# Packed expert and batch numbers, read once and taken apart in registers, in a top-2 MoE kernel

## The reference

```python
out = einsum('btc,oc->bto', x, W_base) + b_base
h = einsum('btc,erc->bter', x, As)
x = x + out + 2.0 * einsum('bter,eor,be->bto', h, Bs, cond_8)

rw = softmax(cond_8); w, sel = top_k(rw, 2); w = w / w.sum(-1)
dense_w = zeros((B, E)).at[arange(B)[:, None], sel].add(w)
mlp = lambda x, g, u, d: (gelu(x @ g) * (x @ u)) @ d      # 128 -> 512 -> 128
x = x + sum_e dense_w[:, e] * mlp(x, gate[e], up[e], down[e]) + mlp(x, shared_gate, shared_up, shared_down)
```

## Time and profile before

| | us |
|---|---|
| median of three runs | 134.96 |
| the profiled execution, its own time | 135.5 |
| its span in the trace | 133.8 |
| TensorE busy in the span | 127.2 (95%) |
| VectorE busy | 88.7 (66%) |
| ScalarE busy | 70.9 (53%) |
| GpSimd busy | 60.2 (45%) |

### The profile page before, as it was taken

How to read it: one execution, slowest core, us unless ns; L and a number is a source line. 1 busy time by engine, 2 the same in 40 slices (tenths; PEclk the granted TensorE clock), 3 DMA queues, 4 the chain that set the end, 5 groups by cost and what they waited for, 6 DMA issues and landing times.

```text
span 133.8 us, 3280 instructions
## 1 busy us (share of the span) xinstructions
PE 127.2 (95%) x869; PEld 114.2 (85%) x869; DVE 88.7 (66%) x172; ACT 70.9 (53%) x134; POOL 60.2 (45%) x110
## 2 busy tenths in 40 slices
PE   6899999999999989996999999999999999999991
PEld 6658787878878869995999999999989999989991
DVE  2668978779977888533376658656855686756732
ACT  3432867976876766120466485657554755711110
POOL 5209384497777644632064543554255504610000
DMA  3898878798000185599345686558799940013822
GB/s 51 245 335 290 287 197 300 227 308 247 12 2 0 39 266 170 157 394 409 144 174 218 238 316 240 193 201 313 260 316 322 347 167 0 0 41 121 248 85 61
DMA packets 14526, 26.56 MB, mean 199 GB/s; under 512 B 2225, under 2 KB 7601, under 8 KB 12977
## 3 DMA queue, kind: packets, MB, share of 16 engines
q1 hardware_dynamic: 14192, 26.35, 58.8%
q10 hardware_dynamic: 320, 0.07, 0.2%
HBM read 12.52 MB, written 1.31 MB: 103 GB/s over the span
## 4 chain that ended last, share of the span: by engine, by line
PE 78%; DVEq 6%; DVE 4%; issue 4%; DMA 3%; ACT 2%; SPq 0%; ACTq 0%
PE bank L999 8%; PE bank L1036 7%; PE bank L1035 7%; PE bank L1034 7%; PE bank L946 5%; PE bank L948 5%; PE bank L947 5%; DVEq L232 5%; PE bank L1016 5%; PE bank L1056 4%; PE bank L962 3%; PE bank L1058 3%; PE bank L1057 3%; PE bank L871 3%; PE bank L964 3%
## 5 line engine op out<-in xcount | busy, mean ns | idle before, releaser
L533 ACT ACTIVATE work<-bank 128x512 f32<-128x512 f32 x48 | 28.7, 598 | 43.0 <-PE bank L1036 18.3
L697 DVE TENSOR_TENSOR bank<-bank,work 128x512 f32<-128x512 f32 x40 | 27.9, 697 | 23.2 <-PE bank L1036 12.5
L714 DVE TENSOR_TENSOR hT_lo<-bank,hT_hi 128x512 fp32r<-128x512 f32 x40 | 27.3, 682 | 1.7 <-issue 0.8
L1034 PE MATMUL bank<-xp,wst 128*128 128x256 f32 x96 | 27.2, 284 | 0.0
L1035 PE MATMUL bank<-xp,wst 128*128 128x256 f32 x96 | 27.2, 283 | 0.0
L1036 PE MATMUL bank<-xp,wst 128*128 128x256 f32 x96 | 27.1, 283 | 0.0
L463 POOL TENSOR_TENSOR wstd<-wexd,wstd 128x512 fp32r<-128x512 f32 x12 | 15.5, 1295 | 23.8 <-ACT wstd L575 23.8
L542 ACT CAST hT_hi<-bank 128x512 fp32r<-128x512 f32 x40 | 23.3, 582 | 2.4 <-DVE bank L697 1.3
L1035 PEld LDWEIGHTS bank<-xp,wst 128*128 128x128 f32 x96 | 18.4, 192 | 0.0
L1036 PEld LDWEIGHTS bank<-xp,wst 128*128 128x128 f32 x96 | 18.4, 192 | 0.0
L1034 PEld LDWEIGHTS bank<-xp,wst 128*128 128x128 f32 x96 | 18.4, 192 | 0.0
(11 more groups left out here) (146 smaller groups left out, 212.7 us busy)
## 6 DMA issues: line engine op xcount, KB each, us to landing
wst<-wex SPq DMA_DIRECT2D x12, 1024.0 KB, 5.0
raw_ex<-n_L_cond_skill_gate_dram SPq DMA_DIRECT2D x8, 256.0 KB, 3.3
raw_ex<-in_L_cond_skill_up_dram SPq DMA_DIRECT2D x8, 256.0 KB, 4.2
sst<-n_L_cond_skill_gate_dram SPq DMA_DIRECT2D x8, 256.0 KB, 3.4
sst<-in_L_cond_skill_up_dram SPq DMA_DIRECT2D x8, 256.0 KB, 4.2
xn<-in_x_dram SPq DMA_DIRECT2D x4, 256.0 KB, 4.6
out_dram<-xT SPq DMA_DIRECT2D x4, 256.0 KB, 2.7
sst<-_L_cond_shared_gate_dram SPq DMA_DIRECT2D x1, 256.0 KB, 4.6
```

The lines of the kernel that those rows point to most:

```text
L533: act.activation(gelu_sb[q], gate_ps[q][:, :], ACT.Gelu_apprx_tanh).then_inc(gelu_done, 1)
L697: dve.tensor_tensor(up_ps[u][:, :], up_ps[u][:, :], gelu_sb[q], ALU.mult).then_inc(h_done, 1)
L714: dve.tensor_tensor(hT_lo[:, q, :], up_ps[u][:, :], f32(hT_hi[:, q, :]), ALU.subtract).then_inc(lo_done, 1)
L1034: pe.matmul(of_c, w_hi, x_hi, start=True, stop=False)
```

## The change

Six small integer tables are made on one partition: `two_b` (two batch numbers in one integer, places of 16), `slot_eb` (expert and both batch numbers of a slot), `six_b` (the batch numbers of three slots), `four_b` (of four singles), `two_e` and `four_e` (the expert numbers of four singles, places of 8). VectorE makes them during group 3 of the shared expert with a memset and seven SCALAR_TENSOR_TENSOR instructions of 1 x 2 to 1 x 16 elements, each counted on a new semaphore `packs`. The engines then read one integer and take the fields out with whole division and remainder in registers. VectorE reads 7 integers in place of 32, TensorE 2 in place of 8, GpSimd 32 in place of 44 (one in `stage_slot`, one in `down_lo`). ScalarE and the DMA queue go on reading `idx`. TensorE's first read waits for `packs` to reach 5, which is the pack behind `gate_lo(5)` in step 14. Its second stands where the last two reads stood, ahead of `down_single(2)`. VectorE's read for singles 4 to 7 stays behind `add_single(3)`, and its read for a turn of three slots stands in half 0 of the first of them.

```diff
@@ -94,6 +94,13 @@
         idx = sb("idx", [1, 64], I32)
+        two_b = sb("two_b", [1, 17], I32)
+        slot_eb = sb("slot_eb", [1, NP], I32)
+        six_b = sb("six_b", [1, 4], I32)
+        four_b = sb("four_b", [1, 2], I32)
+        two_e = sb("two_e", [1, 4], I32)
+        four_e = sb("four_e", [1, 2], I32)
@@ -181,6 +188,7 @@
         lists_ready = sem("lists_ready")
+        packs = sem("packs")
@@ -230,6 +238,12 @@
             return eng.value_load(idx[0:1, bass.ds(n + 32, 1)], min_val=0, max_val=B - 1)
+        def read(eng, table, n, top):
+            return eng.value_load(table[0:1, bass.ds(n, 1)], min_val=0, max_val=top - 1)
+        P_PAD, P_TWO_B, P_SLOT_EB, P_TWO_E, P_FOUR_E, P_FOUR_B, P_SIX_PART, P_SIX_B = range(1, 9)
@@ -451,14 +465,14 @@
             def stage_slot(p, j):
-                for n in range(2):
-                    b = batch_at(pool, 2 * p + n)
+                both = read(pool, slot_eb, p, E * B * B)
+                for n, b in enumerate(((both // B) % B, both % B)):
                     pool.tensor_copy(xp[:, j, :, n, :],
...
             def down_lo(p, j):
-                e0 = down_at(pool, 2 * p)
+                e0 = pool.snap(read(pool, slot_eb, p, E * B * B) // (B * B) * DN)
                 pool.wait_ge(wd_hi_done, p + 1)
@@ -473,6 +487,7 @@
             pool.wait_ge(ex_ulo, E)
+            pool.wait_ge(packs, P_SLOT_EB)
             stage_slot(0, 0)
@@ -726,6 +741,9 @@
+            def pack(out, high, places, low):
+                dve.scalar_tensor_tensor(out, high, float(places), low, ALU.mult, ALU.add).then_inc(packs, 1)
             def shared_group(g):
@@ -753,9 +771,26 @@
                         dve.tensor_reduce(pos[:, :], pos_ke[:, :, :], AXIS_X, ALU.add).then_inc(sort_sum, 1)
+                    if g == 2 and c == 0:
+                        dve.memset(two_b[:, 0:1], 0.0).then_inc(packs, 1)
                     if g == 3 and c == 0:
...
                         dve.tensor_copy(idx[:, :], list_ps[0:1, 0:64]).then_inc(lists_ready, 1)
+                        dve.wait_ge(lists_ready, 2)
+                        dve.wait_ge(packs, P_PAD)
+                        pack(two_b[:, 1:17], idx[:, 32:64:2], B, idx[:, 33:64:2])
+                    if g == 3 and c == 1:
+                        dve.wait_ge(packs, P_TWO_B)
+                        pack(slot_eb[:, :], idx[:, 0:LEFT:2], B * B, two_b[:, 1:1 + NP])
+                        pack(two_e[:, :], idx[:, LEFT:LEFT + NS:2], E, idx[:, LEFT + 1:LEFT + NS:2])
+                    if g == 3 and c == 2:
+                        dve.wait_ge(packs, P_TWO_E)
+                        pack(four_e[:, :], two_e[:, 0:4:2], E * E, two_e[:, 1:4:2])
+                        pack(four_b[:, :], two_b[:, 1 + NP:17:2], B * B, two_b[:, 2 + NP:17:2])
+                    if g == 3 and c == 3:
+                        pack(six_b[:, :], two_b[:, 0:NP:3], B * B, two_b[:, 1:NP:3])
+                        dve.wait_ge(packs, P_SIX_PART)
+                        pack(six_b[:, :], six_b[:, :], B * B, two_b[:, 2:NP:3])
@@ -768,8 +803,11 @@
-            def batches_of(p):
-                return [batch_at(dve, 2 * p + n) for n in range(2)]
+            def of_four(word):
+                return [dve.snap(word // B ** 3), dve.snap(word // (B * B) % B), dve.snap(word // B % B), dve.snap(word % B)]
+            def of_two(word):
+                return [dve.snap(word // B % B), dve.snap(word % B)]
@@ -780,17 +818,21 @@
-            def slot(p, j):
-                adds = not (isinstance(p, int) and p == 0)
-                for n in range(2):
-                    t = 2 * p + (PB + n)
-                    gated(t, n, (PB + 2 * j + n) % 3)
-                    if adds or n == 1:
-                        split_h_lo(t - 1, 1 - n, (PB + 2 * j + n - 1) % 3, split_count(t - 1))
-                    if adds and n == 0:
-                        where = batches_of(p - 1)
-                    if adds and n == 1:
-                        add_slot(p - 1, (j + 2) % NBUF, where)
+            def three_slots(i):
+                for j in range(NBUF):
+                    p = NBUF * i + j
+                    adds = not (isinstance(p, int) and p == 0)
+                    for n in range(2):
+                        t = 2 * p + (PB + n)
+                        gated(t, n, (PB + 2 * j + n) % 3)
+                        if adds or n == 1:
+                            split_h_lo(t - 1, 1 - n, (PB + 2 * j + n - 1) % 3, split_count(t - 1))
+                        if j == 0 and n == 0:
+                            six = read(dve, six_b, i, B ** 6)
+                        if adds and n == 0:
+                            where = of_two(six // B ** (4 - 2 * j))
+                        if adds and n == 1:
+                            add_slot(p - 1, (j + 2) % NBUF, where)
@@ -813,24 +855,21 @@
             sum_group(NG - 1)
-            first = [batch_at(dve, LEFT + s) for s in range(2)]
+            dve.wait_ge(packs, P_SIX_B)
+            first = of_four(read(dve, four_b, 0, B ** 4))
             gated_single(1)
             add_single(0, first[0])
-            first += [batch_at(dve, LEFT + s) for s in range(2, NF)]
             gated_single(2)
             add_single(1, first[1])
-            last = [batch_at(dve, LEFT + s) for s in range(NF, NF + 2)]
             gated_single(3)
...
             add_single(3, first[3])
-            last += [batch_at(dve, LEFT + s) for s in range(NF + 2, NS)]
+            last = of_four(read(dve, four_b, 1, B ** 4))
             dve.wait_ge(sum_done, NG)
-            for p in range(NBUF):
-                slot(p, p)
+            three_slots(0)
             with dve.Fori(1, NP // NBUF) as i:
-                for j in range(NBUF):
-                    slot(NBUF * i + j, j)
-            where = batches_of(NP - 1)
+                three_slots(i)
+            where = of_two(read(dve, two_b, NP, B * B))
             split_h_lo(LB - 1, 1, (LB - 1) % 3, split_count(LB - 1))
@@ -966,12 +1005,17 @@
+            def downs_of(k):
+                word = read(pe, four_e, k, E ** 4)
+                return [word // E ** 3 * DN, word // (E * E) % E * DN, word // E % E * DN, word % E * DN]
             def shared_group(g):
...
                     if NC * g + c == NU - 1:
-                        pe.wait_ge(lists_ready, 2)
-                        first.extend(down_at(pe, LEFT + s) for s in range(NF))
+                        pe.wait_ge(packs, P_FOUR_E)
+                        first.extend(downs_of(0))
                     if g == 0 and c == 2:
@@ -1011,6 +1055,7 @@
                     pe.wait_ge(merged, NG)
+                e0 = pe.snap(e0)
                 pe.wait_ge(h_done, t + 1)
@@ -1090,10 +1135,9 @@
             gate_up_single(2)
-            last = [down_at(pe, LEFT + s) for s in range(NF, NF + 2)]
             down_single(1, first[1])
             gate_up_single(3)
-            last += [down_at(pe, LEFT + s) for s in range(NF + 2, NS)]
+            last = downs_of(1)
             down_single(2, first[2])
```

## The result

The changed kernel takes 133.03 us, the median of four runs between 132.55 and 133.51, against 135.09 us of the kernel before on the same chip. The ratio is 0.984, with a 95% interval of 0.981 to 0.988: 2.1 us (1.6%) faster, where 2.7 were forecast. The profiled executions are 135.5 and 133.25 us, with spans of 133.8 and 131.6.

What follows compares the result with a forecast made beforehand. TensorE was taken to bound the kernel, idling where VectorE or its own stream issued late. Terms +0.35 - 1.3 + 0.3 - 2.0 = -2.65, or -2.7 us, took 134.96 to 132.3, range 131.0 to 133.9.

Steps and rivals of the forecast that it cites:

- the three places: Where TensorE was said to stand empty: at 49 us, at 60 to 64 us, and in the slots.
- (a): TensorE's first read at 49 us: three reads saved, but the wait for the fifth pack takes their place, +0.35 us.
- (b): First singles, 60 to 64 us: reads ahead of TensorE's down matmuls and VectorE's gated product go, slot 0 starts earlier, -1.3 us.
- (c): Start of slot 0: VectorE's read and four fields delay its first product, slot 1's gate matmuls wait, +0.3 us.
- (e): Packs: seven small VectorE instructions of 0.15 us, hidden by idle time or not needed soon, together 0.
- (d): Slots: VectorE's two reads per slot become two fields and one read in three slots, TensorE waits no more, -2.0 us.
- Dear arithmetic: Rival: register division and remainder cost more than a read, slots lose 7 us at 1.5 a field, 139.2 us; chance 0.06.
- Hidden anyway: Rival: streams run far enough ahead that reads cost nothing and only (a) stays, 135.3 us; chance 0.05.
- The next engine: Rival: slow reads of ScalarE and GpSimd hold the slots at half of the loss, 133.5 us; chance 0.14.
- Packs held behind GpSimd: Rival: packs on VectorE wait for GpSimd's `up_lo` near 49 us, delaying the last shared down step, 133.4 us; chance 0.25.

## Why the prediction was right, and where it was not

The direction, the three places and nearly all the sizes held: 132.3 was forecast, 133.03 measured, inside the range of 131.0 to 133.9. Against the trace the sum of -2.65 stands at -2.44. The runs say -2.1, with -1.7 and -2.5 as the ends of their interval, so they allow the sum of the trace but not quite the forecast one; beyond the terms below, no run shows where the difference lies. Term by term:

(a) *TensorE's first read*, forecast +0.35, measured +0.34, by the mechanism given: the wait for the fifth pack and the read behind it, shown by moving both. This term was counted in the forecast and was the price of a place, not of the packing.

(b) *First singles*, forecast -1.3, measured -1.19. TensorE's own reads are 0.64 of it, from the kernel where they are undone. The other 0.55 is VectorE's by subtraction: no run undid VectorE's reads here, and GpSimd's, put back, changed nothing (13.20).

(c) *Slot 0*, forecast +0.3, measured +0.32, for the wrong reason. The step said that VectorE's read and four fields would delay its first product until 2.55 after slot 0 and that slot 1's gate matmuls would wait for it. The product came at 1.92 (65.12 - 63.20), those matmuls did not wait, and the early VectorE read changed nothing. The read took 1.01 and its check 0.19, as forecast; the four fields, 0.76 of the 2.55, were not there, since they are worked out elsewhere (see (e)). What waited was the first down matmul, for ScalarE's read, which my step did not look at because the change does not touch it. The size agreed by chance.

(d) *Slots*, forecast -2.0, measured -1.65 - 0.32 = -1.97. Of this 1.6 comes back when the copies are made small, and 0.35 is the two reads ahead of the last split, which cost as much at 0.30 each. ScalarE and GpSimd were not next once the stage had started.

(e) *Packs*, forecast 0, is confirmed for their own time (0.14 to 0.29 each). The fields are not free where a wait stands ahead. I took them to be worked out behind the read. In the trace they stand in the register arithmetic just ahead of the instruction that uses them, behind its wait for the down product. The rows of `add_slot`'s line after:

```profile
L818 DVEq FUSED_REGOPS  x27: 60/135/232, 71.3 to 118.0; - x27
L818 DVEq ALU_OP  x15: 40/40/40, 80.2 to 115.0; - x15
```

and before:

```profile
L780 DVEq FUSED_REGOPS  x24: 64/86/117, 71.7 to 120.3; - x24
```

In a slot of the loop the arithmetic of the two adds, from its first start to its last end, takes 0.57 (from 79.99 us) in place of 0.29 (from 80.85 us before), so 0.14 per field, close to the 0.15 of the forecast. In the slots nobody waits for that. In the last singles TensorE does, for its own fields: the same row of `down_single`, before and then after,

```profile
L1016 PEldq FUSED_REGOPS  x32: 46/46/51, 53.0 to 130.3; - x32
```

```profile
L1061 PEldq FUSED_REGOPS  x32: 46/46/166, 53.5 to 128.0; - x32
```

and the one ahead of the last single takes 0.098 in place of 0.046, behind the wait for the product. That is the +0.05 of the table: the stretch is 11.03 again with TensorE's reads undone and VectorE's fields still in place, and 11.08 in each of the other six kernels in which TensorE reads packed numbers. This was a missing term, not a wrong one.

The rivals. *Dear arithmetic* is excluded by those rows: a field costs 0.14 where a read costs 0.9. *Hidden anyway* is excluded by the slot reads put back, which cost 1.7 in the slots. *The next engine* did show, at one place only: the start of the slots. *Packs held behind GpSimd* may have happened once, to `two_b`, while two `up_lo` ran on GpSimd (timeline of GpSimd, after):

```profile
42.22 2.55 POOL L385 TENSOR_TENSOR wex<-raw_ex,wex 128x512 fp32r<-128x512 f32 x2 [0.75 <-DVE wex L734]
```

and the pack on VectorE's timeline:

```profile
44.51 0.29 DVE L745 SCALAR_TENSOR_TENSOR two_b<-idx 1x16 int32<-1x16 int32 x1
```

It ended at 44.80, just after GpSimd's at 44.77, and took 0.29, where the others took 0.14 to 0.18. That is consistent with being held. But it is also the longest pack, with 16 elements (`slot_eb` with 12 took 0.18), and it stood in the same place beside GpSimd in all eight kernels that pack, so no run tells the two apart. At 49 us, where it would have cost something, `four_b` started at 49.02 and `up_lo` only at 49.18.

The page's rule that a DMA never contends with a compute engine (the Trainium skill, SBUF — State Buffer, section Who interferes with whom) does not carry over to register reads: with the copies cut to an eighth they took 0.30 instead of 0.87. Beside the loads from DRAM at 46 to 49 us it would have held.

## What to carry to other kernels

A register read holds its engine's stream for its whole latency, so count the reads between two instructions that another engine waits for, the more so while copies inside SBUF run, and read several small numbers in one word where they are many. When a read waits for its data to be made, the place of the wait matters as much as the number of reads: put it behind work that is already queued, and look at what the producer has in front of the last step. When a stage is made to start earlier, look at the reads of the other engines at its start, the untouched ones too, since they may now fall into transfers that had faded before they began.

## What was not expected of the hardware

A register read from SBUF mostly cost 0.26 to 0.32 us in the kernel before when no copy inside SBUF was moving data, beside loads from DRAM too, and up to 1.2 in the traffic of those copies: 1.00 and 1.16 on VectorE, 0.97 and 0.99 on TensorE, and 1.20 on ScalarE in the kernel that reads early. Not every read in that traffic is slow; the 17 of VectorE from 72 to 110 us lie between 0.30 and 1.07, around 0.87. The first read of each engine took longer even where no copy ran: 0.49 on TensorE, 0.55 on VectorE, 0.48 on ScalarE, 0.50 on GpSimd and 0.47 on SyncE, which issues the DMAs. Among the DMAs of the output, at 125.9 and 127.0 us, two of SyncE's reads took 0.80 and 0.64. No run was made on either. The chain of the trace had given VectorE's read as the cause of the wait at the start of the slots; moving each read in turn showed that it was ScalarE's. That chain follows one releaser at each step, and of two that come close together it may name the wrong one.
